# Where the score pieces, the second norm and the routing stand in a hand-written order of 64 positions a slot

## What is computed

```python
def _L0_ffn_ref(x, Wq_pk, pk_keys, Wq, keys_table, values_table, Wo):
    ...
    q = (x @ Wq).reshape(b, n, HEADS, DIM) * DIM ** (-0.5)
    kv_scores, indices = _pk(x, Wq_pk, pk_keys)
    ...
    k = jnp.einsum('bnhk,bnhkd->bnhd', kv_scores, keys_table[ind])
    v = jnp.einsum('bnhk,bnhkd->bnhd', kv_scores, values_table[ind])
    sim = jnp.einsum('bihd,bjhd->bhij', q, k)
    ...
    sim = jnp.where(causal, sim, neg)
    attn = jax.nn.softmax(sim, axis=-1)
    ...
h = _L0_tok_ref(x, L0_tok_W)
h = h + _L0_attn_ref(_layernorm(h, axis=-1), ...)
h = h + _L0_ffn_ref(_layernorm(h, axis=-1), ...)
h = h + _L1_attn_ref(_layernorm(h, axis=-1), L1_attn_Wq, L1_attn_Wk)
h = h + _L1_ffn_ref(_layernorm(h, axis=-1), ...)
```

## Time and profile before

| what | value |
|---|---|
| median of 3 runs | 3223.81 us (3222.35 to 3224.29) |
| the profiled execution | 3221.3 us, span 3219.3 us |
| PE busy | 2771.5 us (86%) |
| DVE busy | 2744.0 us (85%) |
| POOL busy | 2070.0 us (64%) |
| ACT busy | 2032.4 us (63%) |
| granted clock of PE, mean | 0.932 |
| chain that ended last, by line | PE mx_acc L1440 3%, PE mx_O L1452 3%, PE mx_area L1486 2% |

### The profile page before, as it was taken

One profiled execution on the slowest core, in us unless ns is written; L12 is line 12 of the kernel. 1 busy time (PEld: TensorE's weight loads), 2 busy tenths in 40 slices (PEclk: granted clock), 3 DMA queues, 4 the chain that ended last, 5 costly groups with the idle time before them and its releaser, 6 DMA issues. The chain is left out here.

```text
span 3219.3 us, 39268 instructions
## 1 busy us (share of the span) xinstructions
PE 2771.5 (86%) x9722; PEld 1321.3 (41%) x9722; DVE 2744.0 (85%) x9997; ACT 2032.4 (63%) x4498; POOL 2070.0 (64%) x2097
## 2 busy tenths in 40 slices
PE   4883477989898988989898979898999889899887
PEld 2442123434444444444343434444444444444443
DVE  8777998989898989998998999998989999976433
ACT  4222466766767666767676867677766867677522
POOL 4011677777777777777777777777776767777100
PEclk8996698989898989999999999999999999999999
DMA  1001122222222222222221222222222222222000
GB/s 45 27 10 54 43 72 59 64 65 65 64 65 65 65 65 58 71 58 71 59 71 51 78 55 70 58 71 58 72 58 60 64 54 72 58 71 53 9 4 4
DMA packets 85626, 179.86 MB, mean 56 GB/s; under 512 B 40177, under 2 KB 41107, under 8 KB 85398
## 3 DMA queue, kind: packets, MB, share of 16 engines
q0 software_dynamic: 66560, 135.40, 16.0%
q1 hardware_dynamic: 18838, 41.94, 4.2%
HBM read 176.15 MB, written 1.05 MB: 55 GB/s over the span
## 5 line engine op out<-in xcount | busy, mean ns | idle before, releaser
L1412 POOL DMA_INDIRECT mx_G<-in_kv_table,mx_slot_i x2048 | 2009.4, 981 | 697.9 <-issue 577.7
L1440 PE MATMUL mx_acc<-mx_W,mx_table 128*128 128x512 f32 x2048 | 1099.6, 619 | 0.9 <-ACT mx_kvT L1640 0.9
L1802 DVE SCALAR_TENSOR_TENSOR mx_W<-mx_D,mx_W 128x512 f32<-128x512 f32 x1024 | 698.0, 682 | 178.5 <-ACT mx_W L1633 176.9
L1703 ACT ACTIVATE mx_GT<-mx_G,mx_slot_w 128x128 f32<-128x128 f32 x2048 | 759.7, 495 | 58.7 <-DMA mx_G<-in_kv_table,mx_slot_i 51.4
L1633 ACT ACTIVATE mx_W<-mx_D 128x512 f32<-128x512 f32 x1024 | 605.9, 592 | 209.8 <-PE mx_D L1430 205.3
L1440 PEld LDWEIGHTS mx_acc<-mx_W,mx_table 128*128 128x128 f32 x2048 | 407.6, 200 | 176.8 <-issue 96.2
L1657 ACT ACTIVATE mx_PT<-mx_area 128x512 f32<-128x512 f32 x472 | 241.3, 513 | 349.1 <-PE mx_area L1490 192.3
L1430 PE MATMUL mx_D<-mx_U,mx_pick_b 96*128 96x512 bf16 x1024 | 407.4, 398 | 60.1 <-DVE mx_W L1802 58.8
L1452 PE MATMUL mx_O<-mx_PT,mx_KVs 128*65 128x512 f32 (+3 forms) x768 | 310.2, 486 | 2.3 <-ACT mx_PT L1657 1.5
L2028 DVE TENSOR_REDUCE mx_KVs<-mx_GT 128x128 f32<-128x2048 f32 x128 | 291.9, 2280 | 6.0 <-ACT mx_GT L1703 5.9
L1466 PE MATMUL mx_area<-mx_KTa,mx_QTa 64*128 64x512 f32 (+3 forms) x384 | 188.5, 573 | 68.9 <-DVE mx_mx L2046 34.3
(11 more groups left out here) (390 smaller groups left out, 4274.7 us busy)
## 6 DMA issues: line engine op xcount, KB each, us to landing
mx_table<-in_kv_dense SPq DMA_DIRECT2D x64, 512.0 KB, 3.6
mx_G<-in_kv_table,mx_slot_i POOLq DMA_INDIRECT x2048
tz_table<-in_c_dft SPq DMA_DIRECT2D x1, 2048.0 KB, 9.2
tz_table<-in_c_idft SPq DMA_DIRECT2D x8, 256.0 KB, 2.6
out_h<-mx_xc SPq DMA_DIRECT2D x4, 256.0 KB, 2.6
mx_G<-in_c_pick SPq DMA_DIRECT2D x1, 528.0 KB
st_h<-in_tok_W,em_ids POOLq DMA_INDIRECT x32, 2.5
st_keys<-in_pk_keys SPq DMA_DIRECT2D x1, 512.0 KB, 3.9
```

The lines of the kernel that those rows point to most:

```text
L1412: pool.indirect_dma_start(G[g % RING][:, r, :], None, a["kv_table"], bass.IndirectOffsetOnAxis(slot_i[n % 2][:, k, r:r + 1], 0))\
L1440: pe.matmul(acc[:, :], table[:, tile, :], W[c % TILE_RING][:, :], start=(tile == 0), stop=(tile == TILES - 1)).then_inc(applied, 1)
L1703: last = act.activation(GT[:, :, i], G[g % RING][:, i, :], ACT.Copy, scale=slot_w[n % 2][:, k, i:i + 1])
L1802: dve.scalar_tensor_tensor(W[c % TILE_RING][:, :], D_ps[c % 3][:, :], 0.0, W[c % TILE_RING][:, :], ALU.is_ge, ALU.mult).then_inc(w_done, 1)
```

## The change

Only positions change; each engine issues as many instructions as before.

- `PLAIN`: the twelve plain pieces stand at every position 16 to 27 instead of every second one from 16 to 38. `EARLY` follows from 28, `LATER` from 40.
- L1T of sequences 0 and 1: pieces 0 to 7 at the even positions 0 to 14 of stage 2, pieces 8 to 15 at the even positions of stage 3; before at positions 0 to 7 of stage 2 and 8 to 15 of stage 3.
- Extras: neg of head 1 from 42 to 36, the three Y from 43, 47, 60 to 35, 43, 55; the first l1y of sequences 0 and 1 from 10 to 18; l2x from 28, 29 to 39, 41; l2r from 32 to 44.
- `F`: second norm from 22 to 33 (its end from 25 to 36, the square root from 24 to 35), routing from 33, 37, 41, 45 to 45, 49, 53, 57, its exponential from 35 to 47.

```diff
-PLAIN = tuple(range(16, 40, 2))
-EARLY = tuple(range(27, 43, 2))
+PLAIN = tuple(range(16, 28))
+EARLY = (28, 29, 30, 31, 33, 35, 37, 39)
...
-LATER = (44, 45, 46, 48, 49, 50, 52, 53, 54, 56, 57, 58, 60, 61, 62, 63)
+LATER = (40, 41, 43, 44, 46, 47, 49, 50, 52, 53, 55, 56, 58, 59, 61, 62)
...
-            if s == (2 if p < 8 else route_slot(b)):
+            if s == 2 == route_slot(b):
                 return (("L1T", b, 0, p),)
+            if s in (2, 3) and p % 2 == 0 and b < B - 2:
+                return (("L1T", b, 0, 8 * s - 16 + p // 2),)
...
-                 (25, ("neg", n, 0)), (42, ("neg", n, 1)),
-                 (43, ("Y", n, 0, 0)), (47, ("Y", n, 1, 0)), (60, ("Y", n, 0, 1))]
+                 (25, ("neg", n, 0)), (36, ("neg", n, 1)),
+                 (35, ("Y", n, 0, 0)), (43, ("Y", n, 1, 0)), (55, ("Y", n, 0, 1))]
...
-            uses += [(10, ("l1y", b, 0))]
+            uses += [(10 if b >= B - 2 else 18, ("l1y", b, 0))]
...
-            uses += [(19, ("l1y", b, 1)), (28, ("l2x", b, 0)), (29, ("l2x", b, 1)), (32, ("l2r", b))]
+            uses += [(19, ("l1y", b, 1)), (39, ("l2x", b, 0)), (41, ("l2x", b, 1)), (44, ("l2r", b))]
...
-                if (s, p) in ((0, 22), (route_slot(b), 24)):
+                if (s, p) in ((0, 22), (route_slot(b), 35)):
...
-                if (s, p) == (route_slot(b), 35):
+                if (s, p) == (route_slot(b), 47):
...
-                if (s, p) in ((0, 20), (route_slot(b), 22)):
+                if (s, p) in ((0, 20), (route_slot(b), 33)):
...
-                if (s, p) in ((0, 23), (route_slot(b), 25)):
+                if (s, p) in ((0, 23), (route_slot(b), 36)):
...
-                if (s, p) == (route_slot(b), 33):
+                if (s, p) == (route_slot(b), 45):
...
-                if (s, p) == (route_slot(b), 37):
+                if (s, p) == (route_slot(b), 49):
...
-                if (s, p) == (route_slot(b), 41):
+                if (s, p) == (route_slot(b), 53):
...
-                if (s, p) == (route_slot(b), 45):
+                if (s, p) == (route_slot(b), 57):
```

## The result

The changed kernel takes 3247.15 us (median of 4 runs, 3245.18 to 3248.08), the kernel before, measured beside it, 3223.08: ratio 1.0075, 95% interval 1.0059 to 1.0091. It is slower by 24 us, where 11 were forecast; the range of 3204 to 3249 holds it. The profiled execution took 3245.18 us, its span of 3243.2 is 23.9 us above the span of before.

The account below looks back on a forecast made before the run. DVE was taken to bound each slot from position 56 to the handover, PE from there to 56. Slot changes 8.5, layer-1 pieces 1.6 and slot 16 1.0 made 11 us: 3235 us, range 3204 to 3249.

Parts of the forecast that it names:

- Plain pieces before the handover: All twelve precede the first turned piece, where the bound passes from DVE to PE: handover 8.65 us later, gain 2.9 a slot.
- The stretch behind it: PE's work from handover to position 56: -11.5 us, then +3.4 turned pieces, +0.9 Y, +1.3 wait at neg.
- The wait of 4.47 us: PE's wait before the first turned piece: gone or under 2 us, saving 3.1 of 6.26 us at half clock behind it.
- Y and neg: Y at 55 adds 0.9 us on PE before 56; neg at 36 waits 1.3 us for DVE to add the heads.
- 1.7 us later: DVE's delay at position 56, waiting for the Y of 55; counted at five slot changes, 8.5 us.
- Slots 6, 10 and 14: Changes 6 to 7, 10 to 11 and 14 to 15 were priced like other slot changes, 1.7 us each.
- The clock's rival: Short waits at each of the twelve plain-piece positions keep PE's clock falling: +25 us, 3249 us, chance 0.10.
- "Net about 0" for norm and routing: Slots 9 and 13: norm at 33 saves 3.9 us, delays bank release 2.6 and router product 1.5; ends -3.9 and +3.4.
- Layer-1 pieces: Turned layer-1 pieces spread over two slots, first heads at 18: together +0.8 us a pair of slots, 1.6 in all.
- the U wait: U at position 5, before DVE has added the heads of 4: half of 3.21 us, less 0.6, so +1.0.
- Slot 16: PE bounds it, without selection work; each plain piece waits for the maxima of the one before: +1.0 us.
- Slots 2 to 5: GpSimd's gathers take 162 us of each slot's 164 and swallow small gains or losses: 0.

Follow-up runs that it names:

- e7: The changed kernel with the third Y moved back from position 55 to 60; 3241.27 us, ratio 1.0059 to the kernel before.
- e1: The kernel before with only the turned layer-1 pieces spread to every second position and the first layer-1 heads at 18; 3212.28 us, ratio 0.9978.
- e5: e1 with the first norm of sequences 0 to 2 moved from 20 to 33, behind the handover; 3226.77 us, ratio 1.0017 to the kernel before.
- e6: The changed kernel with the first norm of sequences 0 to 2 moved from 20 to 33; 3243.3 us, ratio 1.0069 to the kernel before.
- e4: The changed kernel with second norm, routing and layer-2 products back in their old places; 3241.13 us, ratio 1.0068 to the kernel before.
- e3: The kernel before with only the second norm, the routing and the layer-2 products moved to their new places; 3233.65 us, ratio 1.0047.
- e8: The changed kernel with the routing's four parts at 45, 48, 50, 52 and its exponential at 46; 3247.89 us, ratio 1.0081 to the kernel before.
- e2: The kernel before with only plain pieces, turned pieces, neg and Y at their new places; 3249.71 us, ratio 1.01.
- e9: e1 with the second selection product (qpk) moved from position 31 to 24; 3205.29 us, ratio 0.9966 to the kernel before.

## Why the prediction was right in sign and half in size

*Plain pieces before the handover: right.* "The handover is 8.65 us later": measured 9.2 to 9.3 in slots 7, 11 and 16. The stretch behind it, forecast at -11.5 + 3.4 + 0.9 + 1.3 = -5.9, lost 6.3 to 6.4 in slots 7 and 11. The wait of 4.47 us and all of the half clock behind it went, not half of it; in slot 8, 3.4 us at half clock are left ahead of the handover.

*Y and neg: right.* neg waits 0.95 us for the adding of the heads (forecast 1.3, bounds 0 and 3.2), and DVE waits for Y at 56. A plain slot is 2.8 to 3.4 us longer from 16 to 60 and gives 0.7 back, net 2.1 in slots 11 and 15, against "1.7 us later". e7 shows that Y at 55 is about 0.9 us of it. Slot 7 gave nothing back there but lost 1.0.

*Slots 6, 10 and 14: the step that failed first.* I counted each of these three changes of slot at 1.7 us as if their pieces ran as in slot 8. From 16 to 60 they are 7.1 to 7.2 us longer each, where slots 7, 8, 11 and 12 lose 2.8 to 3.4. The DVE work of their first norm lies among pieces that now follow at every position: PE stands for up to 3.87 us behind it, and DVE, busy for 41.23 of 45.02 us, then waits for the next pieces (idle for 3.8 us, before for 0.6). That it is the norm's place, the crossing of e1, e5, e6 and the change shows (3.5 us with the norm elsewhere, 7.0 with it there). The clock's rival, the one given 0.10, is true here in a small part at most: 13.7 of the 45 us run at half clock, against 6.8 before (with 3.4 behind the handover then, none now), 3.4 us more in all. e4 and e7, in the same order, took 3 us longer for 6.8 us more of half clock; by that it is some 1.5 of the 7.1 us, an estimate. Its sign, a clock below 0.95 in slots 10 and 11, did not come: 0.95 over the whole of slot 10 (0.97 before), 1.00 over slot 11 (0.98 before). Windows of the two slots after, each from its D of position 0 to the next slot's:

```profile
1831.81:2019.31 187.50, 163.20 (x605) 79.57 (x604) 167.18 (x598) 133.74 (x285) 121.52 (x126) 0.95 0.21 58
2019.31:2185.32 166.01, 151.82 (x549) 70.80 (x548) 157.22 (x589) 114.25 (x262) 122.82 (x128) 1.00 0.24 64
```

What the prediction cites from the Trainium skill ("TensorE: Matmul & The Clock Gate", "A second HAM failure mode: psum-queue depth-cycling"), a clock that keeps falling and rising where PE idles briefly between groups of matmuls, agrees with slot 10, where the clock fell three times among the plain pieces, and not with slot 11, where ten waits of 0.15 to 2.23 us left it at 1.00.

*"Net about 0" for norm and routing: the step that failed second.* I took 3.9 us off the one side, put 2.6 and 1.5 on the other for two waits, and nothing for a slow clock in that stretch or for the last part of the routing, which now stands at 57: behind position 56, where by my own account DVE is full. e3 alone costs 14.7 us. Slot 9 against its old place (e4) is -3.6, then +6.2 and +3.7. Timeline after, slot 9, DVE: the norm's first row sum, a mask and the adding of the heads; then PE's neg behind them, after and in e4.

```profile
1752.71 0.69 DVE L178 TENSOR_REDUCE mx_stat<-st_h 128x8 f32<-128x512 f32 x1
...
1756.80 0.68 DVE L1804 SCALAR_TENSOR_TENSOR mx_W<-mx_D,mx_W 128x512 f32<-128x512 f32 x1
...
1761.58 0.85 DVE L2077 SCALAR_TENSOR_TENSOR st_h<-mx_X,mx_rz,st_h 128x64 f32<-128x64 f32 x4
```

```profile
1762.49 1.97 PE L1566 MATMUL mx_X<-mx_ident,mx_mx 128*65 128x128 f32 x8 [3.93 <-DVE st_h L2077]
```

```profile
1772.67 1.09 PE L1566 MATMUL mx_X<-mx_ident,mx_mx 128*65 128x128 f32 x8 [0.96 <-DVE st_h L2077]
```

The norm's way out of DVE's stretch is worth the 3.9 nearly (3.6), and neg's added wait was nearly right too: 3.93 us for 0.96, 3.0 more, where I had 2.6. The 1.5 us at the router's product don't show: PE has no wait there. From the handover to 56 PE stands for 4.06 us, in e4 for 1.19, so the waits are 2.9 of the 6.2 us. The other 3.3 go with the clock: PE is busy for 69.81 us instead of 66.52 with about as many matmuls (261 and 259), at 0.95 instead of 1.00, 7.4 us of the stretch at half clock. 3.4 of these lie behind neg's wait (neg takes 1.97 instead of 1.09 us) and 3.4 behind the router's product, without a wait there. My sum had no slow clock for a stretch into which DVE work is moved, though the earlier trace rows show it behind the old waits. DVE's work in the stretch hardly grew (63.22 us for 62.43, since a part of the routing left it); what costs is where the norm stands, ahead of the adding of the heads for which the bank waits.

Behind 56 DVE is busy for 17.07 of 17.55 us and PE stands for 3.5. Timeline after, slot 9, DVE, first and last of the routing's part at 57:

```profile
1820.50 0.19 DVE L2114 CAST mx_pif<-mx_pi 128x64 f32<-128x64 uint32 x1
...
1822.55 0.23 DVE L2124 TENSOR_TENSOR mx_gate<-mx_comb,mx_r 128x64 f32<-128x64 f32 x1
```

These 2.3 us are paid in full, and DVE begins the combine of 56 2.8 us behind the D of 56, in e4 1.2. e5 and e6 agree for the first norm, and e8 for the routing: what is taken out of one stretch comes back in the other.

*Layer-1 pieces: the step that failed the other way.* Forecast +0.8 a pair, measured -7.0 and -6.9 in e1. I had priced the U wait and the move of the heads against a gain in slot 9 alone, of half its wait. The runs show that both ends are relieved, slot 8's full PE by 2.2 us and slot 9's waits by 4.2. In the changed kernel this gain is eaten up by the norm and the routing: slots 8 and 9 together are +0.9 us in e2, without the layer-1 part, -5.9 in e4, with it, and +0.4 after (slots 12 and 13: -0.7, -5.6 and +0.8).

*Slot 16:* +1.0 forecast, +2.6 measured. *Slots 2 to 5:* forecast 0, and at position 16 of slot 6 the change was 10.5 us ahead (3.4 at 60). e2, e4, e6 and e8, whose order is the same up to there, were ahead by 9.0, 4.0, 10.7 and 9.5, and e1, e3 and e5, with the order of before, by 3.1, 4.2 and -0.4. One order spreads by 6.7 us, but all five kernels of the new one lie 4.0 us or more ahead, so a part of it may be the change's. How much stays open.

So the sum of 11 became 24: some 17 us more in slots 6, 10 and 14 (7.2 to 7.6 each for 1.7), 12 more for norm and routing in slots 9 and 13, and some 15 less for the layer-1 pieces (-14 for +1.6); the three, each worked out from its own pair of kernels, make about +13. The small terms and slots 2 to 5 cancel about. That the range holds the result is thus in part luck: three terms were wrong by 12 to 17 us, and one of them the other way.

**The better version.** e1 alone is faster than both kernels (0.9978), and so is e9 (0.9966, 3205.29 us: 14 us below before by the medians). What carries it is the spreading of the layer-1 pieces (with their first heads at 18, which it needs); the other two parts, each alone, cost time (e2 and e3).

## What to carry to other kernels

Where two engines limit in turns, cut the period at the points where the bound changes hands and price every move in both sums: a block taken out of one stretch was paid again in the other, although the engine that it is on shows idle time there, because the other engine stood behind it (neg's wait) or because a part of it came to lie past the next point (the routing at 57). The same pieces set closer cost twice as much in a slot that already has a long block among them (7.0 us against 3.5). Work that is bunched in one period and missing in the next, as the layer-1 pieces were, was the one gain here, because both periods were relieved. And a stretch into which a change brings a wait has to be priced with a slow clock too: in slot 9 it cost 3.3 us beside 2.9 of waiting.
